# A Mamba block with a ternary layer behind it: the kernel's end is rebuilt

## The reference

```python
def mamba(h, W_in, conv_w, conv_b, Wx, Wdt, bdt, A_log, D, W_out):
    x, z = split(h @ W_in.T)                      # 256 inner channels each
    x = silu(causal_conv(x, conv_w) + conv_b)
    dt, B, C = split(x @ Wx.T)                    # 64, 16, 16
    dt = softplus(dt @ Wdt.T + bdt)
    # for t: s = exp(dt*A)*s + dt*x*B;  y = sum over the 16 states of s*C
    return ((y + x * D) * silu(z)) @ W_out.T

x1 = layernorm(h + mamba(h, fwd) + flip(mamba(flip(h), rev)), eps=1e-5)
mu, var = mean(x1), variance(x1)
xn = (x1 - mu) * rsqrt(var + 1e-3) * ln_gamma + ln_beta
beta = mean(|weight|)
w_q = clip(round(weight / (beta + 1e-5)), -1, 1)  # ternary, 128 x 128
gamma = max(|xn|)                                 # over the whole array
xq = clip(xn * 128 / gamma, -128 + 1e-5, 128 - 1e-5)
out = layernorm(x1 + (xq @ w_q) * (gamma * beta / 128), eps=1e-5)
```

## Time and profile before

| what | value |
|---|---|
| median of 3 runs | 950.46 us (946.37 to 950.92) |
| the profiled execution: own time | 942.61 us |
| the profiled execution: span | 940.8 us |
| TensorE busy, share of the span | 653.1 us, 69% |
| VectorE busy | 848.0 us, 90% |
| ScalarE busy | 591.4 us, 63% |
| GpSimd busy | 844.5 us, 90% |
| mean granted TensorE clock, share of 2.4 GHz | 0.818 |
| last scan ends at | 890.11 us |

### The profile page before, as it was taken

The page is one execution under the profiler, slowest core; times in us unless marked ns, Lnnn a source line. Parts: engine busy times, 40 slices in busy tenths (PEclk is TensorE's granted clock), DMA queues, the critical chain, the costliest instruction groups (busy, mean ns, idle before and its releaser), DMA issues. The chain is left out here.

```text
span 940.8 us, 8196 instructions
## 1 busy us (share of the span) xinstructions
PE 653.1 (69%) x2076; PEld 218.3 (23%) x2076; DVE 848.0 (90%) x910; ACT 591.4 (63%) x966; POOL 844.5 (90%) x408
## 2 busy tenths in 40 slices
PE   6757767859667867768677777768677777556541
PEld 3312121213122222213122222213122222112141
DVE  2289999999999999999999999999999999999945
ACT  3566656666767657666767757666767757565415
POOL 0299999998999999999999999999999999999612
PEclk9978989878889887789779887889689987567656
DMA  2776547554646646654656746554646646650112
GB/s 61 180 206 116 155 90 170 123 111 110 130 138 119 163 89 142 142 101 118 128 149 111 172 90 138 142 106 118 126 128 111 172 90 137 145 101 1 45 46 90
DMA packets 46736, 113.12 MB, mean 120 GB/s; under 512 B 7136, under 2 KB 20448, under 8 KB 46560
## 3 DMA queue, kind: packets, MB, share of 16 engines
q1 hardware_dynamic: 46688, 112.59, 53.4%
HBM read 40.48 MB, written 4.98 MB: 48 GB/s over the span
## 5 line engine op out<-in xcount | busy, mean ns | idle before, releaser
L427 POOL TENSOR_TENSOR dbx<-step_rep,bc_rep 128x1024 f32<-128x1024 f32 x256 | 598.5, 2373 | 12.0 <-DMA step_rep<-step 12.0
L630 ACT ACTIVATE da_ps<-step_rep,neg_a 128x512 f32<-128x512 f32 x512 | 348.3, 687 | 255.5 <-DVE hs L854 250.1
L854 DVE TENSOR_TENSOR_SCAN hs<-da_ps,carry,dbx 128x512 f32<-128x512 f32 x256 | 312.2, 1264 | 13.6 <-ACT da_ps L630 13.6
L854 DVE TENSOR_TENSOR_SCAN hs<-da_ps,dbx 128x512 f32<-128x512 f32 x256 | 296.6, 1203 | 30.6 <-ACT da_ps L630 18.5
L1099 PE MATMUL y_ps<-ch,stack 128*32 128x512 f32 x1024 | 173.9, 755 | 168.0 <-DVE ch L778 104.4
L778 DVE TENSOR_TENSOR ch<-hs,c_ps 128x1024 f32<-128x1024 f32 x176 | 209.8, 1193 | 0.0
L437 POOL TENSOR_TENSOR ch<-hs,bc_rep 128x1024 f32<-128x1024 f32 x80 | 189.4, 2367 | 9.2 <-PE y_ps L1099 5.1
L1090 PE MATMUL c_ps<-x_dbl,select 128*128 128x512 f32 x256 | 185.2, 813 | 0.0
L1045 PE MATMUL pre<-h_t,w_conv 128*128 128x512 f32 x256 | 120.8, 615 | 7.3 <-ACT xs L536 6.8
L1099 PEld LDWEIGHTS y_ps<-ch,stack 128*32 128x32 f32 x1024 | 24.2, 118 | 272.6 <-issue 177.2
L1090 PEld LDWEIGHTS c_ps<-x_dbl,select 128*128 128x128 f32 x256 | 48.2, 235 | 141.2 <-issue 129.1
(11 more groups left out here) (127 smaller groups left out, 447.9 us busy)
## 6 DMA issues: line engine op xcount, KB each, us to landing
step_rep<-step SPq DMA_DIRECT2D x128, 512.0 KB, 8.3
bc_rep<-bc_rows SPq DMA_DIRECT2D x64, 512.0 KB, 5.9
h_in<-in_L_attn_hidden_states SPq DMA_DIRECT2D x4, 512.0 KB, 8.6
h_res<-in_L_attn_hidden_states SPq DMA_DIRECT2D x4, 512.0 KB, 8.9
out<-hs SPq DMA_DIRECT2D x4, 512.0 KB, 3.2
x_rows<-xn SPq DMA_DIRECT2D x7, 256.0 KB, 7.9
dbx<-x_rows SPq DMA_DIRECT2D x1, 1536.0 KB, 6.7
bc_rows<-x_dbl SPq DMA_DIRECT2D x16, 64.0 KB
```

Of the source, the lines that this page charges most:

```text
L427: nc.gpsimd.tensor_tensor(dbx[:, n % RING], dtx_rep[:, r], b_rep[:, s % 2, k, :].unsqueeze(1).to_broadcast([P, 2, CHUNK]), ALU.mult).then_ ...
L630: nc.scalar.activation(da_ps[:, half % DA_BANKS, :], dt_rep[:, r, e, :], ACT.Exp, scale=neg_a[:, half_of(unit), 2 * (unit % 2) + e, g, k:k ...
L854: nc.vector.tensor_tensor_scan(in_scan_order(hs[:, n % RING, e, :], s), in_scan_order(da_ps[:, (2 * n + e) % DA_BANKS, :], s), in_scan_ord ...
```

## The change

`POOL_C` for the last group of each batch becomes (1, 4, 8, 11, 14): VectorE takes unit 13's product and GpSimd unit 14's. All else concerns the end.

- The last gate goes by halves (`gate_half`): the first after unit 11's scans, the second after the last sum. TensorE puts the residual into `pre` with a product by the identity, adds the first half of the output product, then the last units, then the second half. The addition of `residual` goes; statistics read PSUM.
- The norm for `xn` comes first, with a `pow` of four columns; VectorE (not ScalarE) writes `xhat`. GpSimd then makes the norm for `x1` with a second `pow` of four columns (`last_norms`).
- TensorE puts `x1` into all eight banks ahead, by products with the identity (`start_last`), four of them ahead of the transposes. The transposes go to `da_ps[:, 2]`.
- `scale` is multiplied into the ternary weight (`w_q_scaled`), so that the product adds the finished term to `x1` in PSUM; VectorE's addition L935 goes. The small factors come before the clips with fewer waits.
- `x1_rows` is loaded back into `bc_rep[:, 0]`, 24 tiles of it during the last group.
- There are five pieces of 2, 2, 2, 1 and 1 banks (`LAST_PIECES`), statistics and final normalisation read PSUM, VectorE normalises the last piece, and SP stores five times.

```diff
-POOL_C = ((1, 4, 8, 11, 13),) * NG
+POOL_C = ((1, 4, 8, 11, 13),) * (NG - 1) + ((1, 4, 8, 11, 14),)
...
-        x1_last = dbx[:, :, :, :].rearrange("p a b t -> p (a b t)").rearrange("p (j m) -> p j m", m=P)
+        x1_last = bc_rep[:, 0].rearrange("p k c t -> p (k c t)").rearrange("p (j m) -> p j m", m=P)
+        w_q_scaled = ch[:, 2, 0, 0:P]
+        LAST_ORDER = (0, 1, 2, 3, 4, 5, 7, 6)
+        LAST_PIECES = ((0, 1), (2, 3), (4, 5), (7,), (6,))
...
+                    if last and s == NG - 1:
+                        sp.wait_ge(dbx_ready, UNITS * group)
+                        sp.wait_ge(ch_pool, pool_c(b, s))
+                        sp.wait_ge(x1_stored, 16 * (2 * BATCH - 2))
+                        sp.dma_start(x1_last[:, 0:TILES - 2 * TT, :], x1_rows[:, 0:TILES - 2 * TT, :]).then_inc(x1_in, 16)
                     if s == NG - 1:
                         store_x1(b, 0)
...
+            def last_norms():
+                pool.wait_ge(last_spread, 1)
+                nc.gpsimd.tensor_tensor(rstd[:, 1, :], spread_of[:, 1, :], half[:, 0:TT], ALU.pow).then_inc(last_rstd, 1)
+                nc.gpsimd.tensor_scalar(spread_of[:, 0, :], mv[:, :, 1], LN1_EPS, None, ALU.add).then_inc(spread_ready, 1)
+                nc.gpsimd.tensor_scalar(neg_mean[:], mv[:, :, 0], -1.0, None, ALU.mult).then_inc(spread_ready, 1)
+                pool.wait_ge(spread_ready, 3 * (2 * BATCH - 1) + 2)
+                nc.gpsimd.tensor_tensor(rstd[:, 0, :], spread_of[:, 0, :], half[:, 0:TT], ALU.pow).then_inc(rstd_ready, 1)
+                pool.wait_ge(rstd_ready, 2 * BATCH)
+                nc.gpsimd.tensor_tensor(bias[:, 0, :], rstd[:, 0, :], neg_mean[:], ALU.mult).then_inc(bias_ready, 1)
...
-            gate(BATCH - 1, 3)
-            residual(BATCH - 1, 1)
-            statistics(BATCH - 1, 1)
+            gate_half(BATCH - 1, 1)
+            dve.wait_ge(o_ps, 2 * BATCH)
+            for j in range(TT):
+                nc.vector.bn_stats(stats[:, j, :], pre[:, j * P:(j + 1) * P]).then_inc(stats_ready, 1)
             mean(BATCH - 1, 1)
...
+            clip(LAST_ORDER[0])
+            dve.wait_ge(small_dve, small[0])
+            dve.wait_ge(wq_ready, 1)
+            nc.vector.tensor_scalar(w_q_scaled, w_q[:], scale, None, ALU.mult).then_inc(wq_scaled, 1)
+            for j in LAST_ORDER[1:]:
+                clip(j)
...
+            def last_output_half(a):
+                if a == 0:
+                    pe.wait_ge(h_res_ready, 16 * BATCH)
+                    pe.wait_ge(xn_sb, 2 * BATCH - 1)
+                    nc.tensor.matmul(pre[:], ident[:], h_res[:, 0:TT, :].rearrange("p t m -> p (t m)"), start=True, stop=False)
+                    pe.wait_ge(g_half, 1)
...
+            last_output_half(0)
             add_units(BATCH - 1, NG - 1, UNITS - 2)
-            output_product(BATCH - 1, 1, True)
-            transpose_norm(BATCH - 1, 1)
+            last_output_half(1)
+            pe.wait_ge(ch_vector, NVC * BATCH)
+            pe.wait_ge(scanned, 2 * UNITS * NG * BATCH)
+            for j in (0, 1, 4, 5):
+                start_last(j)
+            pe.wait_ge(xn_ready, TT * 2 * BATCH)
+            for t in range(TT):
+                ins = nc.tensor.transpose(da_ps[:, 2, t * P:(t + 1) * P], xhat[:, t, :], ident[:])
+            ins.then_inc(xn_ps, 1)
+            for j in (2, 3):
+                start_last(j)
             pe.wait_ge(xn_sb, 2 * BATCH)
+            pe.wait_ge(x1_ready, TT * 2 * BATCH)
+            start_last(7)
+            start_last(6)
+            pe.wait_ge(wq_scaled, 1)
```

More of the change, by code:

```diff
@@ L392, in _ @@
             batches(sp, batch)
-            sp.wait_ge(scanned, 2 * UNITS * NG * BATCH)
             sp.wait_ge(x1_stored, 16 * (2 * BATCH - 1))
-            kept = slice(0, TILES - 2 * TT), slice(TILES - TT, TILES)
-            for tiles in kept:
-                sp.dma_start(x1_last[:, tiles, :], x1_rows[:, tiles, :]).then_inc(x1_in, 16)
-            for c in range(BATCH):
-                sp.wait_ge(final_ready, c + 1)
-                tiles = slice(c * TILES // BATCH, (c + 1) * TILES // BATCH)
-                sp.dma_start(out_tiles[:, tiles, :], z_last[:, tiles, :]).then_inc(stored, 16)
-            sp.wait_ge(stored, 16 * BATCH)
+            sp.dma_start(x1_last[:, TILES - TT:, :], x1_rows[:, TILES - TT:, :]).then_inc(x1_in, 16)
+            for c in range(len(LAST_PIECES)):
+                if c == len(LAST_PIECES) - 1:
+                    sp.wait_ge(final_dve, 1)
+                else:
+                    sp.wait_ge(final_ready, c + 1)
+                sp.dma_start(out_tiles[:, piece_tiles(c), :], z_last[:, piece_tiles(c), :]).then_inc(stored, 16)
+            sp.wait_ge(stored, 16 * len(LAST_PIECES))
         @block.gpsimd
@@ L789, in gate, with gate_half @@
                 nc.vector.tensor_tensor(gated[:], y_ps[:], silu_z[:, :, chunk_of(s)], ALU.mult).then_inc(g_ready, 1)
+            def gate_half(b, a):
+                dve.wait_ge(summed, UNITS * (NG * b + 3) + UNITS // DT * (a + 1))
+                dve.wait_ge(silu_z_ready, 2 * b + 2)
+                dve.wait_ge(o_ps, 2 * b + 1)
+                nc.vector.tensor_tensor(gated[:, a, :], y_ps[:, a, :], silu_z[:, a, chunk_of(3)],
+                                        ALU.mult).then_inc(g_ready if a else g_half, 1)
             def residual(b, h_e):
@@ L873, in batch @@
                             gate(b - 1, 3)
+                        if last and s == NG - 1 and n == 11:
+                            gate_half(b, 0)
                         if closing and n == CLOSING["residual"]:
@@ new lines, in _, with last_statistics @@
+            small[0] += 1
+            clip(LAST_ORDER[0])
[4 more added lines that the diff above has]
+                clip(j)
+            def last_statistics(c):
+                for j in LAST_PIECES[c]:
+                    dve.wait_ge(out_ps, LAST_ORDER.index(j) + 1)
+                    for m in range(TT):
+                        nc.vector.bn_stats(stats_last[:, j * TT + m, :], last_bank(j)[:, m * P:(m + 1) * P]).then_inc(stats_ready, 1)
+                done = sum(len(piece) for piece in LAST_PIECES[:c + 1])
+                dve.wait_ge(stats_ready, TT * (2 * BATCH + done))
+                tiles = piece_tiles(c)
+                for m in range(tiles.start, tiles.stop):
+                    ins = nc.vector.bn_aggr(mv_last[:, m, :], stats_last[:, m, :])
@@ L946, in last_sum @@
                 ins.then_inc(mv_last_ready, 1)
                 dve.wait_ge(mv_last_ready, 2 * c + 1)
-                nc.vector.tensor_scalar(mv_last[:, t0:t0 + per, 1], mv_last[:, t0:t0 + per, 1], LN1_EPS, None,
+                nc.vector.tensor_scalar(mv_last[:, tiles, 1], mv_last[:, tiles, 1], LN1_EPS, None,
                                         ALU.add).then_inc(mv_last_ready, 1)
             def last_bias(c):
-                t = slice(c * per, (c + 1) * per)
+                t = piece_tiles(c)
@@ L956, in last_bias @@
                                                ALU.mult, ALU.mult).then_inc(bias_last_ready, 1)
-            for c in range(BATCH):
-                last_sum(c)
+            for c in range(len(LAST_PIECES)):
+                last_statistics(c)
                 if c:
                     last_bias(c - 1)
-            last_bias(BATCH - 1)
+            last_bias(len(LAST_PIECES) - 1)
+            dve.wait_ge(bias_last_ready, len(LAST_PIECES))
+            for j in LAST_PIECES[-1]:
+                for t in range(TT):
+                    m = j * TT + t
+                    ins = nc.vector.tensor_scalar(z_last[:, m, :], last_bank(j)[:, t * P:(t + 1) * P],
+                                                  rstd_last[:, m:m + 1], bias_last[:, m:m + 1], ALU.mult, ALU.add)
+            ins.then_inc(final_dve, 1)
         @block.tensor
@@ L1225, in _ @@
                     k = (j * TT + t) * P
[L1226 removed]
+                    ins = nc.tensor.matmul(bank[:, t * P:(t + 1) * P], xn_t[:, k:k + P], w_q_scaled, start=False, stop=t == TT - 1)
                 ins.then_inc(out_ps, 1)
```

114 lines of the change are left out of this document (56 added, 58 removed).

## The result

Before: 950.17 us median (946.37 to 950.92, four runs). Changed: 935.98 us (933.48 to 937.15, four runs). The ratio is 0.9894, 95% interval [0.9849, 0.9939]. A second measurement gave 936.58 (six runs) against 945.58 (eleven runs), ratio 0.9892 [0.9852, 0.9933]. So by the ratio the change gains 1.1%, some 10 us. The medians themselves differ by 14.2 us in the first measurement (a quotient of 0.9851, near the interval's lower end) and by 9.0 in the second: single executions of one kernel scatter by several us. The forecast was 8.7 us off an own time of 942.61, a ratio of 0.9908, which lies in both intervals; the range in time, 936.5 to 947.0, missed the first median by 0.5 us and holds the second.

A forecast was written before the change was run, and what follows sets the result against it. No engine bounds the end: it is one chain of short steps, its all-reduce set by GpSimd's preceding work. Terms -0.9 - 2.57 - 2.2 - 2.85 - 0.2 = -8.7 take the median 950.46 to 941.7 us; range 936.5 to 947.0.

The forecast's parts named there:

- paragraph (b) of the prediction's first part: 904.6 to 910.83: the all-reduce waits for a 5.8 us switch of GpSimd's code, starting when its preceding work ends.
- Fast rival: Ahead of the all-reduce: the 1.24 us is a plain delay, not a code switch; start 2.6 sooner, 939.1; chance 0.10.
- Cold TensorE: At the end, TensorE stays at 1.2 GHz through the new calls; ScalarE ends 4.0 us later, 945.7; chance 0.17.
- Slower rival: At the loop's hand-overs, GpSimd's product 14 makes the next dbx late, 3.64 us a batch; 953.6; chance 0.06.
- Loop, -0.9: At three hand-overs, the moved product fills VectorE's stall and the next scans start sooner: 3 x 0.3 us gained.
- Last sum, +0.75: In the last group, the first gate half and new TensorE work make the last sum end 0.75 us later.
- Gate, output product, residual: Behind the last sum: halved gate -0.57, output product with half its records -2.4, residual add gone -0.72 us.
- Statistics from PSUM, +0.2 for four and +0.25 for eight: VectorE's statistics reading PSUM at the end: 0.2 us more for four, 0.25 for eight following each other.
- Norms, +0.17: GpSimd's last norms, with two pows of four columns at 0.93 us each, take 3.1 us instead of 2.94.
- ScalarE's rest, -2.85: Final normalisation: ScalarE does 28 tiles at 0.4 us without gaps, 11.05 us where it was 13.9.
- Stores, -0.2: At the end, two stores of 256 KB, issued 0.4 us apart, instead of one of 512 KB: 0.2 us gained.
- The code switch runs a second time, covered by 1.5 us: Before the first final pow: a second 5.8 us switch after the all-reduce ends 1.5 us before that pow is due.

The follow-up runs named there:

- the last version: The changed kernel with the last norms off GpSimd, VectorE normalising two banks instead of one, and six stores: 929.26 us, ratio 0.9815 to the kernel before.
- the filled cover: The changed kernel with five unneeded maxima of 1024 columns on VectorE ahead of the last maximum: last scan's end to span's end 41.54 us, against 39.29.
- the free GpSimd: The changed kernel with the last norms moved off GpSimd, square root on ScalarE, reciprocal and biases on VectorE: 932.00 us.
- `POOL_C` alone: The kernel before with only the last group's POOL_C changed, unit 14 for 13: 945.55 us, beside one run of before at 941.88.
- the whole gate: The changed kernel with gate and output product whole again behind the last sum: last scan's end to span's end 40.56 us, against 39.29.

## Why the prediction was right, point by point

The ratio came out as forecast, and the main reading, in paragraph (b) of the prediction's first part, held. GpSimd's end of work sets the all-reduce, with 5.82 us between them; the work between them is under a cover of 3.8 us. The all-reduce starts 3.17 sooner, where the forecast had 2.57. Two kernels (and the last version), in which the maximum is late or GpSimd is free early, show the all-reduce 0.14 behind the maximum. The Trainium skill ("GPSIMD Engine Reference", 2.1 Instruction dispatch) gives about 6 us for the first call of a newly loaded kernel; the runs agree (5.82 to 6.21 in nine executions), and show beyond it that the time runs while the engine waits.

- *Fast rival* (plain delay): fallen, by the filled cover and by the free GpSimd. *Cold TensorE*: fallen; the clock was 1.00 through the identity calls. Where it did fall, with the calls behind the transposes, the cost was 0.2 and not the rival's 4.0. *Slower rival* (GpSimd paces the loop): right that GpSimd sets the pace, wrong in place and size; what is given back is 0.3 us and not 3.6, at the next group's tenth unit and by way of the norm's bias, not of a late dbx.
- *Loop, -0.9*: wrong. The step that failed is "the next scans start when their input is there": I followed the gain one scan far and took the earlier trace rows, with only two waits of a scan for GpSimd's dbx, for room. The wait at the next group's tenth unit stands under ScalarE's name, two links from GpSimd. In the changed kernel and in `POOL_C` alone all six hand-overs gave the 0.3 back.
- *Last sum, +0.75*: measured +0.37; the sum took 1.07 at the full granted clock, where I had taken a value between cold and warm.
- *Gate, output product, residual*: right in size. The product's term was right for a partly wrong reason, as the whole gate showed: the clock gives 1.73 of it.
- *Statistics from PSUM, +0.2 for four and +0.25 for eight*: measured +0.02 and +0.05, the lower bound. The Trainium skill ("VectorE: DVE Perf Modes", the TRN2 errata) has 62 cycles more for a PSUM source; the estimates of 0.26 and 1.0 us worked out from it are not borne out for these statistics. VectorE's last normalisation does show such a price: four tiles took 1.36 us from PSUM here and 1.11 from SBUF in the kernel with the sums on VectorE, 62 ns each. This and clips without a pause give the 0.73 by which ScalarE starts sooner than forecast: the first statistics began 4.39 behind the all-reduce's end (forecast 4.6), the two pieces took 5.13 (5.65).
- *Norms, +0.17*: measured +0.37; pow of four 1.01 and 1.04, forecast 0.93. The cost does go mostly by elements, but not wholly.
- *ScalarE's rest, -2.85*: the mis-sized term with the most weight, -4.01. I used 0.40 a tile from the earlier trace rows, a source in SBUF (28 of them would be 11.2, not the 11.05 of the sum); from PSUM 28 in a row take 9.89, which is 0.353 each. From SBUF they take 0.392 each in a row, 10.98 for the two stretches of the kernel with the sums on VectorE.
- *Stores, -0.2*: wrong in sign, +0.44. I compared the last store alone; with the stores closer together, the last two have to wait for the third one's transfers. That is 0.37 of the 0.44, and the smaller size brought nothing.
- *"The code switch runs a second time, covered by 1.5 us"*: it does run, but takes 7.1 us or more and not 5.8, and had no room: the first pow was 0.2 late in the changed kernel. Much faster statistics would have gained little there: in no execution did the way back take less than 7.04.

The errors of single terms (+0.90 loop, +0.64 stores; -0.60 up to GpSimd's last norm, -0.73 and -1.16 behind it) partly cancel; that the sum is within 1 us of the measured stages is partly luck. The median of the changed kernel lies lower than the forecast, 936.0 against 941.7. The loop's scatter is in both medians: that of before alone moved from 950.2 to 945.6 between the two measurements, and the places of the last group's first scan lay up to 9.4 us apart in kernels with the same loop. The list of terms can't foresee it; the low end of the range, 936.5, was too near, by 0.5 us. What causes these steps in the loop stays open; no run was made on it.

## What to carry to other kernels

Where an engine's idle time before a special instruction has no releaser, look for where its preceding work ended: such a time can be covered, so bring that end forward, and look at the way back behind it too. A gain at a loop's hand-over must be followed through the whole next group, also across two engines, until either it is still there or a wait has grown by just as much. When an engine at the end gets faster, look at what its outputs queue for: here it cost 0.37 to 0.54 us of the gain at the stores.

## What the runs showed of the hardware that was not expected

- GpSimd's way back from the all-reduce to ordinary instructions takes about 7.1 us and up to 7.82, longer than the way in (5.82 to 6.21). The 7.08 is put down to "issue", with the input there all along; where the pow started at 7.04, its input came only at 6.95.
- pow on GpSimd: 1.67 us for 128x8, 1.01 to 1.04 for 128x4, a multiply of either 0.20. A square root of 128x8 on ScalarE took 0.21.
- The same sixteen products of 128x128 took 3.78 us behind an idle TensorE (granted clock 0.50) and 2.05 behind a busy one (1.00).
- VectorE's statistics from PSUM, one behind the other, cost 6 ns each more than from SBUF, while its normalisation of 128 columns costs 62 ns more; ScalarE's normalisation of 128 columns is 0.04 us cheaper from PSUM.
- Stores of 512 KB: 0.9 us from issue to first transfer, 1.95 us of transfer, 0.8 to the end of the span.
